# Gated cross-attention: the attended memory computed already turned, and softmax shares applied ahead of the turn

## The chip, the cores and the metric

The kernel runs on one core of a Trainium2 chip. The metric is the device time of one execution in microseconds (us). Three runs of the kernel before are shown by their median; a further, profiled execution has a time of its own.

## What is computed

For each of 32 batches there are 112 rows of `x` (512 numbers each) and 375 memory rows (256 numbers each).

```
memory_proj    = memory @ W_mem.T                          # 375 x 512
scores         = x @ memory_proj.T / sqrt(512)             # 112 x 375
attn           = softmax(scores)
memory_context = attn @ memory_proj                        # 112 x 512
gate           = sigmoid(concat(x, memory_context) @ W_gate.T + b_gate)
fused          = x + gate * memory_context
out            = fused * rsqrt(mean(fused**2) + 1e-6) * norm_w
```

The kernel never forms `memory_proj`. It computes q = x W_mem (112 x 256), scores = q memory.T, the attended memory am = attn memory (112 x 256), and from am both the context (am W_mem.T) and the gate's second half (am times a weight product made once).

## The kernel before, in words

Every operand of a product is split into two float32r parts, a rounded "high" and the remainder "low". A product is three kinds of matmul into one accumulator: high by high, high left by low right, and low left by high right. ScalarE (ACT) writes the high parts by a copy with rounding, VectorE (DVE) or GpSimd (POOL) writes the low ones by a subtraction. The left operand of `pe.matmul(out, left, right)` is the one that is loaded into TensorE (PE) and stays there; the right one streams through, one column after the other.

Work is done in 4 groups of 8 batches, the middle two in a hardware loop. The 896 rows of a group make 7 tiles of 128 rows for gate, context and output, and three column units (256, 320, 320) for q. There is no scheduler: each engine has its own written order of work, and semaphores join them. On PE, batch `b` of a group is

1. `score(b)`: 6 matmuls of 376 columns (done at the end of the group before for b = 0)
2. `after_scores`: fillers from `fillers(g, b, last)`, from b = 3 on `gate_x(b-1)`, 12 matmuls of 512 columns; 9 of them in the last batch of the last group
3. `probs_turn(b)`: 3 transposes of the exponentials (112 x 384) into the bank `pT_ps`
4. `after_probs`: fillers, from b = 2 on `gate_am(b-2)`, 6 matmuls of 512 columns
5. `attend(b)`: 9 matmuls. The left operand is a 128 x 112 block of the turned exponentials, the right one a 128 x 256 block of memory; the sum is am, 112 x 256, in `am_bank`
6. `after_am`: fillers, from b = 2 on `context(b-2)`, 6 matmuls of 512 columns
7. `am_turn(b)`: 2 transposes of am, which ACT has copied to SBUF and scaled by `share` (one over the row's sum), back into `am_bank`

On DVE the order of batch b is `gate_context(b-3)`, `amT_low(b-1)`, `maximum(b)` (row maximum and its scaling), `fuse(b-3)`, `shares(b)` (the reciprocal of the row sums), `pT_low(b)`, q remainders, `norm(b-3)`, `add_bias(b-2)`. Between groups it is ... `fuse(6)`, `maximum` of the next group's batch 0, a q remainder, `norm(6)`, and then the next group's `shares(0)`. ACT computes the exponential and its row sum, then a square, memory splits, `pT_hi`, `am`, a tanh and `amT_hi`. POOL computes the memory and x remainders and the inverse root for `norm`.

`probs_turn` waits for `probs_ready` (ACT's exponential) alone; `share` is needed only at the copy of am.

Of the kernel before, what the change touches and what calls it, by code (L numbers as in the profile page):

```python
# [24 lines left out]
F32R = mybir.dt.float32r  # L25
ACT = mybir.ActivationFunctionType
# [54 lines left out]
def build_gated_cross_attention(nc, x_d, xT_d, mems_d, first_d, wmT_d, wgT_d, b_d, nw_d, out_d):  # L81
    ctx = ExitStack()
    with ctx:
# [25 lines left out]
        memT_hi, memT_lo = (sb(f"memT_{s}", [P, 2, EC, KEVEN], F32R) for s in ("hi", "lo"))  # L109
        mem_hi, mem_lo = (sb(f"mem_{s}", [P, 2, KC, E], F32R) for s in ("hi", "lo"))  # L110
        probs = sb("probs", [ROWS, 2, KPAD])
        pT_hi, pT_lo = (sb(f"pT_{s}", [P, 2, KC, ROWS], F32R) for s in ("hi", "lo"))
        am = sb("am", [ROWS, E])
        x_rows = sb("x_rows", [P, X_SLOTS, D])
        work = sb("work", [P, 8, D])
        z, late_h, y = work[:, 0:2], work[:, 2:4], work[:, 4:6]
# [34 lines left out]
        late_ps = [ctx_ps, gate_ps[LAST_SLOT - 1]]  # L151
        scores = score_ps[0:ROWS, 0:KEVEN]
        probsT = pT_ps[:, 0:KC * ROWS].rearrange("p (c n) -> p c n", c=KC)
        am_ps = am_bank[0:ROWS, 0:E]
        amT_ps = am_bank[:, E:E + EC * ROWS].rearrange("p (c n) -> p c n", c=EC)


        wmT_loaded, vectors_loaded = sem("wmT_loaded"), sem("vectors_loaded")
# [19 lines left out]
        scores_done, top_ready, shift_ready = sem("scores_done"), sem("top_ready"), sem("shift_ready")  # L178
        probs_ready, share_ready = sem("probs_ready"), sem("share_ready")
        pT_done, pT_hi_ready, pT_lo_ready = sem("pT_done"), sem("pT_hi_ready"), sem("pT_lo_ready")  # L180
        am_done, am_ready = sem("am_done"), sem("am_ready")
        amT_done, amT_hi_ready, amT_lo_ready = sem("amT_done"), sem("amT_hi_ready"), sem("amT_lo_ready")
        gate_x_done, gate_done, ctx_done = sem("gate_x_done"), sem("gate_done"), sem("ctx_done")
        z_ready, tanh_ready, u_ready, h_ready = sem("z_ready"), sem("tanh_ready"), sem("u_ready"), sem("h_ready")
        meansq_ready, guarded_ready, rstd_ready = sem("meansq_ready"), sem("guarded_ready"), sem("rstd_ready")
# [89 lines left out]
        def _(pe):  # L275
# [50 lines left out]
                low_lefts(scores, q, memory).then_inc(scores_done, 1)  # L326

            def probs_turn(g, b):
                pe.wait_ge(probs_ready, GROUP * g + b + 1)
                for c in range(KC):  # L330
                    mm = pe.transpose(probsT[:, c], probs[:, b % 2, c * P:(c + 1) * P], ident[0:ROWS, 0:ROWS])  # L331
                mm.then_inc(pT_done, 1)

            def attend(g, b):
                turned = [(pT_hi[:, b % 2, c], pT_lo[:, b % 2, c]) for c in range(KC)]
                memory = [(mem_hi[:, b % 2, c], mem_lo[:, b % 2, c]) for c in range(KC)]
                pe.wait_ge(pT_hi_ready, GROUP * g + b + 1)
                pe.wait_ge(mem_hi_ready, GROUP * g + b + 1)
                pe.wait_ge(mem_lo_ready, GROUP * g + b + 1)
                if b > 0:  # L340

                    pe.wait_ge(amT_lo_ready, GROUP * g + b)
                high_lefts(am_ps, turned, memory)
                pe.wait_ge(pT_lo_ready, GROUP * g + b + 1)
                low_lefts(am_ps, turned, memory).then_inc(am_done, 1)

            def am_turn(g, b):
                pe.wait_ge(am_ready, GROUP * g + b + 1)
                for c in range(EC):
                    mm = pe.transpose(amT_ps[:, c], am[:, c * P:(c + 1) * P], ident[0:ROWS, 0:ROWS])  # L350
                mm.then_inc(amT_done, 1)

            def gate_x(g, t, part=WHOLE):
# [39 lines left out]
            def fillers(g, b, last):  # L393

                if b == 0:
                    return ([(q_piece, 1, 1)], [(gate_x, 0, OPEN)], [(q_piece, 2, 0, OPEN)])
                if b == 1:
                    return ([(q_piece, 2, 0, CLOSE), (gate_x, 0, CLOSE)], [(gate_x, 1, OPEN)], [(q_piece, 2, 1, OPEN)])
                if b == GROUP - 1 and last:
                    return ([(gate_x, b - 1, (0, 3))], [(gate_am, b - 2)], [(context, b - 2, OPEN)])  # L400
                gates = [(q_piece, 2, 1, CLOSE), (gate_x, 1, CLOSE)] if b == 2 else [(gate_x, b - 1)]
                return (gates, [(gate_am, b - 2)], [(context, b - 2)])

            def group(g, last, first=False):


                for b in range(GROUP):
                    after_scores, after_probs, after_am = fillers(g, b, last)
                    if first and b == 0:
                        after_scores = []  # L410
                    if b > 0:
                        score(g, b)
                    for what, *which in after_scores:
                        what(g, *which)
                    probs_turn(g, b)
                    for what, *which in after_probs:
                        what(g, *which)
                    attend(g, b)
                    for what, *which in after_am:
                        what(g, *which)  # L420
                    am_turn(g, b)
                if last:
                    context(g, TILES - 2, CLOSE)
                    gate_x(g, TILES - 1, (3, 4))
                    gate_am(g, TILES - 1)
                    for cols, bank in zip(HALVES, late_ps):
                        context(g, TILES - 1, cols=cols, bank=bank, late=True)
                else:
                    q_piece(g + 1, 0, 0)
                    q_piece(g + 1, 0, 1)  # L430
                    gate_am(g, TILES - 1)
                    context(g, TILES - 1)
                    score(g + 1, 0)
                    q_piece(g + 1, 1, 0)
# [72 lines left out]
        def _(act):  # L507
# [86 lines left out]
            def group(g, last, first=False):  # L594
                for b in range(GROUP):
                    ahead = not last or b + 1 < GROUP
                    after = (g, b + 1) if b + 1 < GROUP else (g + 1, 0)
                    if first and b == 1:
                        wga_high(0)
                    elif b > 0 and ahead:  # L600
                        split_memT(*after)
                    if b > 0:
                        exponentials(g, b)
                    if b >= 3:
                        square(g, b - 3)
                    if first and b == 1:
                        wga_high(1)
                    elif b > 0 and ahead:
                        split_mem(*after)
                    if b in (1, 2) and not (first and b == 1):  # L610
                        q_high(g, 2, b - 1)
                    act.wait_ge(pT_done, GROUP * g + b + 1)
                    high(pT_hi[:, b % 2], probsT).then_inc(pT_hi_ready, 1)
                    if first and b == 1:
                        split_memT(*after)
                        q_high(g, 2, 0)
                        wmT_high(0)
                    if b == 0:
                        if not first:
                            split_memT(*after)  # L620
                            q_high(g, 1, 1)
                        else:
                            wgx_high(2)
                            wgx_high(3)
                        split_mem(*after)
                    if not last and b in SPLIT_AT:

                        unit = SPLIT_AT.index(b)
                        act.wait_ge(gate_x_done, TILES * g + last_tile_of(unit) + 1)
                        split_xT(g + 1, unit)  # L630

                    act.wait_ge(share_ready, GROUP * g + b + 1)
                    act.wait_ge(am_done, GROUP * g + b + 1)
                    act.activation(am[:], am_ps, ACT.Copy,  # L634
                                   scale=share[:, b % 2:b % 2 + 1]).then_inc(am_ready, 1)
                    if b >= 2:
                        tanh(g, b - 2)
                    act.wait_ge(amT_done, GROUP * g + b + 1)
                    high(amT_hi[:, :, b * ROWS:(b + 1) * ROWS], amT_ps).then_inc(amT_hi_ready, 1)
                    if first and b == 1:  # L640
                        wmT_high(1)
                        split_mem(*after)
# [22 lines left out]
        def _(dve):  # L665
# [17 lines left out]
            def shares(g, b):  # L683
                s = slice(b % 2, b % 2 + 1)
                dve.wait_ge(probs_ready, GROUP * g + b + 1)
                dve.reciprocal(share[:, s], total[:, s]).then_inc(share_ready, 1)

            def pT_low(g, b):
                dve.wait_ge(pT_hi_ready, GROUP * g + b + 1)
# [2 lines left out]
            def amT_low(g, b):  # L692
                cols = slice(b * ROWS, (b + 1) * ROWS)
                dve.wait_ge(amT_hi_ready, GROUP * g + b + 1)
                low(amT_lo[:, :, cols], amT_ps, amT_hi[:, :, cols]).then_inc(amT_lo_ready, 1)

            def add_bias(g, t, cols=ALL):
                dve.wait_ge(vectors_loaded, 32)
# [85 lines left out]

            def group(g, last, first=False):
                for b in range(GROUP):
                    if b >= 3:
                        gate_context(g, b - 3)
                    if b >= 1:
                        amT_low(g, b - 1)  # L790
                    if b > 0:
                        maximum(g, b)
                    if first and b == 1:
# [23 lines left out]
                if last:  # L817
# [10 lines left out]
                    for cols in HALVES:  # L828
                        norm(g, TILES - 1, cols, late_h[:, LAST_SLOT])
                else:  # L830
                    gate_context(g, TILES - 2)
                    amT_low(g, GROUP - 1)
                    fuse(g, TILES - 2)
                    q_low(g + 1, 0, 0)
                    norm(g, TILES - 2)
# [123 lines left out]
```

## Time and profile before

| | |
|---|---|
| median of 3 runs | 299.44 us (297.44 to 299.56) |
| profiled execution, its own time | 297.53 us |
| its span, first to last instruction | 295.7 us |
| granted TensorE clock, mean over the span | 0.994 |
| PE matmuls | 287.5 us busy, 97% of the span, 1638 instructions |
| PE weight loads | 250.9 us, 85%, beside the matmuls |
| ACT / DVE / POOL busy | 59% / 53% / 53% |

Busy times are sums over the span. PE records overlap one another, since a matmul's record lasts until its results are out, so the spacing of their starts or of their ends is what they cost, not their duration. An engine that is half busy costs nothing unless PE waits for it.

### The profile page before, as it was taken

Reading aid. Unit: us, or ns where it says so; the run is one execution under the profiler, and the core shown is the slowest. Engines: PE = TensorE matmul, PEld = TensorE weight load, DVE = VectorE, ACT = ScalarE, POOL = GpSimd, SP = SyncE. Lnnn points to the kernel's source line nnn. Section 1 sums busy time; section 2 is a strip of 40 time slices with the busy share of each in tenths; the row PEclk is TensorE's granted clock in tenths of the full one; section 3 lists DMA queues with packets and bytes.
Section 4 is the critical chain, followed back from the end, with each engine's and each line's share of the span. In section 5 each row is a group of like instructions: output and inputs, shape, how many; then the busy total and the mean of one; then the engine's idle time right before and its main releaser. Section 6 shows DMA issues by size and latency. Waiting matters only on the chain.

```text
span 295.7 us, 4924 instructions
## 1 busy us (share of the span) xinstructions
PE 287.5 (97%) x1638; PEld 250.9 (85%) x1638; DVE 155.4 (53%) x327; ACT 173.1 (59%) x364; POOL 156.3 (53%) x132
## 2 busy tenths in 40 slices
PE   6999999999999999999999999999999999999991
PEld 3989888888989988888889988888889998888881
DVE  3897555455554255545464344555456334555555
ACT  4886657667537555657636555757744656555442
POOL 0002765858717545859824645775861954445302
PEclk9999999999999999999999999999999999999997
DMA  7997257576532734656561551757562333552101
GB/s 273 423 349 248 95 207 266 176 254 189 173 112 56 261 109 151 230 170 199 164 222 71 155 200 46 258 168 265 176 212 71 137 111 105 178 176 73 38 35 71
DMA packets 15426, 50.83 MB, mean 172 GB/s; under 512 B 1712, under 2 KB 1968, under 8 KB 15152
## 3 DMA queue, kind: packets, MB, share of 16 engines
q1 hardware_dynamic: 15408, 50.60, 50.7%
q8 instruction: 10, 0.16, 0.2%
q14 instruction: 8, 0.07, 0.1%
HBM read 43.25 MB, written 7.34 MB: 171 GB/s over the span
## 4 chain that ended last, share of the span: by engine, by line
PE 93%; DMA 3%; ACT 1%; DVE 1%; issue 0%; DVEq 0%; POOL 0%; POOLq 0%; SPq 0%
PE gate_ps L279 13%; PE gate_ps L281 13%; PE gate_ps L286 13%; PE ctx_ps L279 5%; PE ctx_ps L286 5%; PE ctx_ps L281 5%; PE am_bank L286 4%; PE am_bank L281 4%; PE am_bank L279 4%; PE q_ps L286 4%; PE q_ps L279 4%; PE q_ps L281 4%; PE score_ps L279 4%; PE score_ps L286 4%; PE score_ps L281 4%; PE pT_ps L331 3%
## 5 line engine op out<-in xcount | busy, mean ns | idle before, releaser
L853 POOL TENSOR_TENSOR memT_lo<-mems_raw,memT_hi 128x752 fp32r<-128x752 f32 x30 | 54.5, 1815 | 88.2 <-ACT memT_hi L509 88.2
L853 POOL TENSOR_TENSOR mem_lo<-mems_raw,mem_hi 128x768 fp32r<-128x768 f32 x30 | 56.4, 1881 | 3.5 <-ACT mem_hi L509 3.5
L634 ACT ACTIVATE am<-am_bank,share 112x256 f32<-112x256 f32 x32 | 15.2, 476 | 47.0 <-PE am_bank L286 47.0
L667 DVE TENSOR_TENSOR pT_lo<-pT_ps,pT_hi 128x336 fp32r<-128x336 f32 x32 | 16.2, 508 | 47.1 <-ACT pT_hi L509 47.0
L706 DVE SCALAR_TENSOR_TENSOR ctx_ps<-work,ctx_ps 128x512 f32<-128x512 f32 x26 | 18.1, 697 | 40.9 <-PE ctx_ps L286 40.9
L534 ACT ACTIVATE probs<-score_ps,shift 112x375 f32<-112x375 f32 x32 | 18.4, 575 | 27.5 <-DVE shift L681 27.5
L279 PE MATMUL gate_ps<-wgx_hi,xT_hi 128*128 128x512 f32 x112 | 32.4, 398 | 0.0
L281 PE MATMUL gate_ps<-wgx_lo,xT_hi 128*128 128x512 f32 x112 | 31.7, 392 | 0.0
L286 PE MATMUL gate_ps<-wgx_hi,xT_lo 128*128 128x512 f32 x112 | 31.6, 391 | 0.0
L509 ACT ACTIVATE memT_hi<-mems_raw 128x752 fp32r<-128x752 f32 x32 | 26.4, 826 | 0.9 <-DMA mems_raw<-in_mems 0.9
L509 ACT ACTIVATE mem_hi<-mems_raw 128x768 fp32r<-128x768 f32 x32 | 26.8, 837 | 0.0
L871 POOL TENSOR_TENSOR guarded<-meansq,eps 128x1 f32<-128x1 f32 x27 | 5.1, 191 | 39.9 <-ACT work L541 39.9
L853 POOL TENSOR_TENSOR xT_lo<-xT_raw,xT_hi 128x1280 fp32r<-128x1280 f32 (+1 forms) x9 | 25.0, 2776 | 0.0
L281 PEld LDWEIGHTS gate_ps<-wgx_lo,xT_hi 128*128 128x128 f32 x112 | 21.0, 188 | 4.6
L286 PEld LDWEIGHTS gate_ps<-wgx_hi,xT_lo 128*128 128x128 f32 x112 | 21.0, 188 | 4.6
L721 DVE SCALAR_TENSOR_TENSOR work<-ctx_ps,rstd,norm_w 128x512 f32<-128x512 f32 x26 | 19.4, 744 | 3.8 <-POOL rstd L873 3.7
L279 PEld LDWEIGHTS gate_ps<-wgx_hi,xT_hi 128*128 128x128 f32 x112 | 19.8, 188 | 1.8
L546 ACT ACTIVATE work<-work 128x512 f32<-128x512 f32 (+1 forms) x29 | 17.6, 610 | 5.9 <-DVE work L700 5.9
L509 ACT ACTIVATE amT_hi<-am_bank 128x224 fp32r<-128x224 f32 x32 | 11.5, 358 | 16.3 <-PE am_bank L350 16.3
L667 DVE TENSOR_TENSOR amT_lo<-am_bank,amT_hi 128x224 fp32r<-128x224 f32 x32 | 12.3, 386 | 15.9 <-ACT amT_hi L509 15.9
L679 DVE TENSOR_REDUCE top<-score_ps 112x1 f32<-112x375 f32 x32 | 17.5, 548 | 5.7 <-PE score_ps L286 5.7
L700 DVE TENSOR_TENSOR work<-gate_ps,b_gate 128x512 f32<-128x512 f32 (+1 forms) x29 | 19.2, 664 | 0.9 <-PE gate_ps L286 0.6
(128 smaller groups left out, 663.9 us busy)
## 6 DMA issues: line engine op xcount, KB each, us to landing
mems_raw<-in_mems SPq DMA_DIRECT2D x32, 760.0 KB, 4.5
x_rows<-in_x SPq DMA_DIRECT2D x28, 256.0 KB, 4.9
out<-work SPq DMA_DIRECT2D x27, 256.0 KB, 5.1
xT_raw<-in_xT SPq DMA_DIRECT2D x8, 640.0 KB, 5.7
xT_raw<-in_xT SPq DMA_DIRECT2D x3, 512.0 KB, 5.2
work<-in_wgT SPq DMA_DIRECT2D x1, 1024.0 KB, 7.7
x_rows<-in_wgT SPq DMA_DIRECT2D x1, 1024.0 KB, 10.8
first_raw<-in_first SPq DMA_DIRECT2D x1, 512.0 KB, 3.8
```

The lines of the kernel that those rows point to most:

```text
L279: pe.matmul(out, l_hi, r_hi, start=first and i == 0, stop=False)
L281: pe.matmul(out, l_hi, r_lo, start=False, stop=False)
L286: mm = pe.matmul(out, l_lo, r_hi, start=False, stop=last and i == len(lefts) - 1)
L509: return act.activation(out, in_, ACT.Copy)
L534: act.activation(probs[:, b % 2, 0:KEYS], scores[:, 0:KEYS], ACT.Exp, bias=shift[:, b % 2:b % 2 + 1], scale=D ** -0.5, accum_out=total[:, ...
L546: act.activation(z[:, t % 2, cols], z[:, t % 2, cols], ACT.Tanh, scale=0.5).then_inc(tanh_ready, 1)
L667: return dve.tensor_tensor(out, in_, high.bitcast(F32), ALU.subtract)
L679: dve.tensor_reduce(top[:, s], scores[:, 0:KEYS], AX.X, ALU.max).then_inc(top_ready, 1)
L700: dve.tensor_tensor(z[:, t % 2, cols], gate_ps[t % 2][:, cols], b_gate[:, cols], ALU.add).then_inc(z_ready, 1)
L706: dve.scalar_tensor_tensor(out=u[:, cols], in0=z[:, t % 2, cols], scalar=1.0, in1=bank[:, cols], op0=ALU.add, op1=ALU.mult).then_inc(u_rea ...
L721: dve.scalar_tensor_tensor(out=y[:, t % 2, cols], in0=h[:, cols], scalar=rstd[:, t % 2:t % 2 + 1], in1=norm_w[:, cols], op0=ALU.mult, op1= ...
L853: return pool.tensor_tensor(out, in_, high.bitcast(F32), ALU.subtract)
```

## The change

The attended memory is computed with memory as the left (loaded) operand, so it comes out as 256 x 112 already turned, in two blocks `e` of 128. The high and low turned exponentials stand side by side in one tile `pT`, so that one matmul by the high memory streams both, 224 columns; one by the low memory streams the high ones alone, 112 columns. Per batch these are 12 matmuls in place of 9, and `am_turn` with its copy on ACT is gone. The product by the low exponentials lies in a second part of the bank and is added by DVE: `amT_low` becomes two instructions. The division by the row sum moves ahead of the transposes: `shares` gets a DVE instruction that multiplies the 112 x 375 exponentials in place, and `probs_turn` waits for that. `attend` waits for the low parts of `pT` before its first matmul. Fillers of batches 1 and 2 are placed anew, and `amT_low` goes ahead of `gate_context` on DVE.

```
             def probs_turn(g, b):
-                pe.wait_ge(probs_ready, GROUP * g + b + 1)
+                pe.wait_ge(shared_ready, GROUP * g + b + 1)
...
             def attend(g, b):
-                pe.wait_ge(pT_hi_ready, GROUP * g + b + 1)
+                slot = b % 2
+                pe.wait_ge(pT_lo_ready, GROUP * g + b + 1)
...
-                high_lefts(am_ps, turned, memory)
-                pe.wait_ge(pT_lo_ready, GROUP * g + b + 1)
-                low_lefts(am_ps, turned, memory).then_inc(am_done, 1)
-
-            def am_turn(g, b):
-                pe.wait_ge(am_ready, GROUP * g + b + 1)
-                for c in range(EC):
-                    mm = pe.transpose(amT_ps[:, c], am[:, c * P:(c + 1) * P], ident[0:ROWS, 0:ROWS])
+                for e in range(EC):
+                    es = slice(e * P, (e + 1) * P)
+
+                    def by_high(c, first=False, last=False):
+                        return pe.matmul(amT_parts[:, e], mem_hi[:, slot, c, es], pT[:, slot, c], start=first, stop=last)
+
+                    def by_low(c):
+                        pe.matmul(amT_parts[:, e, 0], mem_lo[:, slot, c, es], pT[:, slot, c, 0], start=False, stop=False)
+
+                    by_high(0, first=True)
+                    for c in range(KC - 1):
+                        by_low(c)
+                        if c > 0:
+                            by_high(c)
+                    by_low(KC - 1)
+                    mm = by_high(KC - 1, last=True)
                 mm.then_inc(amT_done, 1)
...
                 if b == 1:
-                    return ([(q_piece, 2, 0, CLOSE), (gate_x, 0, CLOSE)], [(gate_x, 1, OPEN)], [(q_piece, 2, 1, OPEN)])
+                    return ([(q_piece, 2, 0, CLOSE), (gate_x, 0, CLOSE), (q_piece, 2, 1, OPEN)], [(gate_x, 1, OPEN)], [])
+                if b == 2:
+                    return ([(q_piece, 2, 1, CLOSE), (gate_x, 1, CLOSE), (gate_am, 0)], [(context, 0)], [])
...
-                gates = [(q_piece, 2, 1, CLOSE), (gate_x, 1, CLOSE)] if b == 2 else [(gate_x, b - 1)]
-                return (gates, [(gate_am, b - 2)], [(context, b - 2)])
+                return ([(gate_x, b - 1)], [(gate_am, b - 2)], [(context, b - 2)])
...
-                    act.wait_ge(share_ready, GROUP * g + b + 1)
-                    act.wait_ge(am_done, GROUP * g + b + 1)
-                    act.activation(am[:], am_ps, ACT.Copy,
-                                   scale=share[:, b % 2:b % 2 + 1]).then_inc(am_ready, 1)
...
                 dve.reciprocal(share[:, s], total[:, s]).then_inc(share_ready, 1)
+                dve.wait_ge(share_ready, GROUP * g + b + 1)
+                dve.tensor_scalar(probs[:, b % 2, 0:KEYS], probs[:, b % 2, 0:KEYS], share[:, s], None,
+                                  ALU.mult).then_inc(shared_ready, 1)
...
-                low(amT_lo[:, :, cols], amT_ps, amT_hi[:, :, cols]).then_inc(amT_lo_ready, 1)
+                low(amT_rest[:], amT_ps, amT_hi[:, :, cols]).then_inc(amT_rest_ready, 1)
+                dve.wait_ge(amT_rest_ready, GROUP * g + b + 1)
+                dve.tensor_tensor(amT_lo[:, :, cols], amT_rest[:], amT_parts[:, :, 1], ALU.add).then_inc(amT_lo_ready, 1)
...
                 for b in range(GROUP):
+                    if b >= 1:
+                        amT_low(g, b - 1)
                     if b >= 3:
                         gate_context(g, b - 3)
-                    if b >= 1:
-                        amT_low(g, b - 1)
```

## Rows read from the trace of the kernel before

**Rows 1.** The page, chain that ended last: shares of the span by engine.

```profile
PE 93%; DMA 3%; ACT 1%; DVE 1%; issue 0%; DVEq 0%; POOL 0%; POOLq 0%; SPq 0%
```

**Rows 2.** The chain in order of time, 158 to 163 us: start, us, what.

```profile
158.32 0.29 PE pT_ps L331 x3
...
160.01 0.35 PE am_bank L279 x3
...
161.94 0.20 PE am_bank L350 x2
```

**Rows 3.** Weight loads in time, 158.0 to 162.3 us: start, us of the run, count.

```profile
157.87 0.19 PEld L286 LDWEIGHTS q_ps<-xT_hi,wm_lo 128*128 128x128 f32 x1
...
158.36 0.30 PEld L279 LDWEIGHTS gate_ps<-wgx_hi,xT_hi 128*128 128x128 f32 x2
```

**Rows 4.** The chain in order of time, 146 to 149 us.

```profile
147.83 0.49 PE q_ps L279 x4
```

**Rows 5.** All engines in time, a steady batch (b = 4), 185.7 to 190.4 us.

```profile
185.99 0.55 DVE L679 TENSOR_REDUCE top<-score_ps 112x1 f32<-112x375 f32 x1 [0.16 <-PE score_ps L286]
186.13 1.81 POOL L853 TENSOR_TENSOR memT_lo<-mems_raw,memT_hi 128x752 fp32r<-128x752 f32 x1 [3.32 <-ACT memT_hi L509]
186.57 0.15 DVE L681 TENSOR_SCALAR shift<-top 112x1 f32<-112x1 f32 x1
...
187.46 0.16 DVE L686 RECIPROCAL share<-total 112x1 f32<-112x1 f32 x1
...
188.56 0.45 PE L331 MATMUL pT_ps<-ident,probs 112*128 112x112 f32 x3
...
189.53 0.51 DVE L667 TENSOR_TENSOR pT_lo<-pT_ps,pT_hi 128x336 fp32r<-128x336 f32 x1 [1.91 <-ACT pT_hi L509]
...
190.25 0.40 PE L279 MATMUL am_bank<-mem_hi,pT_hi 128*112 128x256 f32 x2
```

**Rows 6.** All engines in time, start of a group, 158.0 to 159.4 us.

```profile
158.16 0.45 PE L331 MATMUL pT_ps<-ident,probs 112*128 112x112 f32 x3
158.32 0.75 DVE L721 SCALAR_TENSOR_TENSOR work<-ctx_ps,rstd,norm_w 128x512 f32<-128x512 f32 x1 [0.18 <-POOL rstd L873]
...
158.99 0.15 DVE L686 RECIPROCAL share<-total 112x1 f32<-112x1 f32 x1
```

**Rows 7.** All engines in time, batches 2 and 3, 174 to 181 us.

```profile
174.75 0.52 PE L286 MATMUL am_bank<-mem_hi,pT_lo 128*112 128x256 f32 x3
...
176.74 0.69 DVE L706 SCALAR_TENSOR_TENSOR ctx_ps<-work,ctx_ps 128x512 f32<-128x512 f32 x1 [1.80 <-PE ctx_ps L286]
...
177.34 0.38 DVE L667 TENSOR_TENSOR amT_lo<-am_bank,amT_hi 128x224 fp32r<-128x224 f32 x1
...
180.45 0.45 PE L331 MATMUL pT_ps<-ident,probs 112*128 112x112 f32 x3
```

**Rows 8.** All engines in time, first group, 18 to 34.5 us.

```profile
18.81 0.45 PE L331 MATMUL pT_ps<-ident,probs 112*128 112x112 f32 x3
...
19.53 0.15 DVE L686 RECIPROCAL share<-total 112x1 f32<-112x1 f32 x1
...
25.92 0.45 PE L331 MATMUL pT_ps<-ident,probs 112*128 112x112 f32 x3
...
26.57 0.15 DVE L686 RECIPROCAL share<-total 112x1 f32<-112x1 f32 x1
...
27.75 1.81 POOL L853 TENSOR_TENSOR memT_lo<-mems_raw,memT_hi 128x752 fp32r<-128x752 f32 x1 [26.27 <-ACT memT_hi L509]
...
28.46 1.66 DVE L667 TENSOR_TENSOR wmT_lo<-first_raw,wmT_hi 128x512 fp32r<-128x512 f32 x1
...
31.67 0.68 DVE L667 TENSOR_TENSOR wmT_lo<-first_raw,wmT_hi 128x512 fp32r<-128x512 f32 x1
...
33.32 0.51 PE L331 MATMUL pT_ps<-ident,probs 112*128 112x112 f32 x3
```

**Rows 9.** All engines in time, last batch, 281.0 to 282.5 us.

```profile
281.26 0.16 DVE L686 RECIPROCAL share<-total 112x1 f32<-112x1 f32 x1
...
281.68 0.45 PE L331 MATMUL pT_ps<-ident,probs 112*128 112x112 f32 x3
```

More of the change, by code:

```diff
@@ L111, in build_gated_cross_attention @@
         probs = sb("probs", [ROWS, 2, KPAD])
-        pT_hi, pT_lo = (sb(f"pT_{s}", [P, 2, KC, ROWS], F32R) for s in ("hi", "lo"))
-        am = sb("am", [ROWS, E])
+        pT = sb("pT", [P, 2, KC, 2, ROWS], F32R)
+        pT_hi, pT_lo = pT[:, :, :, 0], pT[:, :, :, 1]
+        amT_rest = sb("amT_rest", [P, EC, ROWS])
         x_rows = sb("x_rows", [P, X_SLOTS, D])
@@ L153, in build_gated_cross_attention @@
         probsT = pT_ps[:, 0:KC * ROWS].rearrange("p (c n) -> p c n", c=KC)
-        am_ps = am_bank[0:ROWS, 0:E]
-        amT_ps = am_bank[:, E:E + EC * ROWS].rearrange("p (c n) -> p c n", c=EC)
+        amT_parts = am_bank[:, 0:EC * 2 * ROWS].rearrange("p (c s n) -> p c s n", c=EC, s=2)
+        amT_ps = amT_parts[:, :, 0]
         wmT_loaded, vectors_loaded = sem("wmT_loaded"), sem("vectors_loaded")
@@ L180, in build_gated_cross_attention @@
         pT_done, pT_hi_ready, pT_lo_ready = sem("pT_done"), sem("pT_hi_ready"), sem("pT_lo_ready")
-        am_done, am_ready = sem("am_done"), sem("am_ready")
-        amT_done, amT_hi_ready, amT_lo_ready = sem("amT_done"), sem("amT_hi_ready"), sem("amT_lo_ready")
+        shared_ready, amT_done, amT_rest_ready = sem("shared_ready"), sem("amT_done"), sem("amT_rest_ready")
+        amT_hi_ready, amT_lo_ready = sem("amT_hi_ready"), sem("amT_lo_ready")
         gate_x_done, gate_done, ctx_done = sem("gate_x_done"), sem("gate_done"), sem("ctx_done")
@@ L334, in attend @@
             def attend(g, b):
-                turned = [(pT_hi[:, b % 2, c], pT_lo[:, b % 2, c]) for c in range(KC)]
-                memory = [(mem_hi[:, b % 2, c], mem_lo[:, b % 2, c]) for c in range(KC)]
-                pe.wait_ge(pT_hi_ready, GROUP * g + b + 1)
+                slot = b % 2
+                pe.wait_ge(pT_lo_ready, GROUP * g + b + 1)
                 pe.wait_ge(mem_hi_ready, GROUP * g + b + 1)
@@ L420, in group @@
                         what(g, *which)
-                    am_turn(g, b)
                 if last:
@@ L830, in group @@
                 else:
+                    amT_low(g, GROUP - 1)
                     gate_context(g, TILES - 2)
-                    amT_low(g, GROUP - 1)
                     fuse(g, TILES - 2)
```

## The prediction, as it went on record

> **What bounds the kernel now.** The first view to read is the chain that ended last: 93% of the span is PE [rows 1]. The second is that chain in order of time, which shows PE's groups of work back to back: three transposes in 0.29 us, three attending matmuls in 0.35 us, two transposes of am in 0.20 us [rows 2]. So a PE matmul costs its spacing (0.117 us for an attending one, 0.10 for a transpose), and whatever lengthens PE's stream or makes PE wait lengthens the kernel. The third view is the timeline of all engines at the places where the change adds a wait: there the question is how long before PE's transposes the reciprocal of the row sums is done [rows 5, 6, 8, 9].
>
> **PE's own stream.** Removed per batch: 9 attending matmuls, 3 x 0.35 = 1.05 us, and 2 transposes, 0.20 us [rows 2], together 1.25 us. Added: 12 matmuls, 6 of 224 and 6 of 112 columns. In columns this is a gain: 2016 in place of 2304 plus 224. But all twelve need a new load of 128 columns. The loads are the limit: two loads that stand directly behind one another take 0.30 us where one takes 0.19 [rows 3], so a load starts no sooner than 0.11 us after the one before it, whatever streams beside it. The matmuls of the q product that stream 256 columns past a 128-column load come every 0.49 / 4 = 0.12 us [rows 4]. A 224-column matmul lies near that row, a 112-column one near the bare load; I take the middle, 0.115, so 12 x 0.115 = 1.38 us, or +0.13 per batch and +4.2 us for 32. The bounds are 12 x 0.11 = 1.32 (+2.2 us in all) and 12 x 0.12 = 1.44 (+6.1 us).
>
> The spacing in rows 3 speaks against what a page would let one hope. The Trainium skill, "TensorE: Matmul & The Clock Gate", section "Back-to-back issue gap", gives about 81 ns per matmul for a sustained stream of load and matmul pairs at 128 columns. With that for the six narrow ones and 0.11 for the others the attending would take 1.15 us, a gain of 3.3 us in all; the two loads of this trace stand at 0.11 us, and I go by them.
>
> **The multiply ahead of the transposes.** The trace has no such instruction (112 x 375, SBUF to SBUF, a scalar per row). From below its cost is that of a one-column one, 0.15 us; from above that of the reduction over the same 375 columns, 0.55 us [rows 5]. I take the upper one, since its size is the same. Add 0.03 between two dependent DVE instructions (186.54 to 186.57 [rows 5]) and 0.11 from a release to the first transpose: I estimate that as 0.05 for the semaphore and 0.06 for a load that can't be hidden, since the run of three at 33.32, which came straight out of a wait, has 0.51 us and not 0.45 [rows 8, 5]. So the first transpose can come no sooner than 0.69 us after the end of the reciprocal.
>
> The Trainium skill, "VectorE: DVE Perf Modes", section "Mode 2x_2P", says that a float32 tensor_scalar from SBUF takes two elements per cycle. As an estimate from that page's 0.96 GHz this makes 0.15 + 0.20 = 0.35 us, and the whole sum 2.0 us less; no row here shows it.
>
> - Steady batches (4 to 7 of a group, and batch 7 in all but the last): the reciprocal ends at 187.62, so the transposes may start at 188.31; they start at 188.56 [rows 5]. Cost 0, with 0.25 to spare. The cover is the 2.8 us of `gate_x`; without it every batch would wait. If DVE and POOL exclude each other while this multiply runs, it starts at POOL's end, 187.94, and the transposes at 188.60, 0.04 late. That such a hold exists is in the first group: one DVE subtraction of two SBUF tensors took 1.66 us and its twin 0.68, the long one while POOL was in an instruction until 29.56 [rows 8].
> - Start of groups 1 to 3: the transposes now run at 158.16, before `share` exists. DVE is in `norm(6)` from 158.32 to 159.07, which waited for POOL, and the reciprocal ends at 159.14 [rows 6]. New start 159.83, so PE waits 1.67 us, three times: 5.0 us. Queued behind PE's wait are the gate's first half and `attend`, nothing that could run instead.
> - Batch 0 of the first group: reciprocal done at 19.68 (DVE is in x's remainder before it), transposes at 18.81 [rows 8]; new 20.37, 1.6 us.
> - Batch 1 of the first group: reciprocal done 26.72, transposes 25.92 [rows 8]; the moved q filler (6 matmuls of 320 columns, 6 x 0.12 x 320 / 256 = 0.90 us by rows 4) puts PE's arrival at 26.82, and the new start is 27.41: 0.6 us. Batches 1 and 2 of later groups get 0.9 and 1.39 us more cover than they had and don't wait.
> - Batch 3, all groups: `context(0)` no longer stands between `attend(2)` and `score(3)`, and `amT_low(2)`, now twice 0.38, with `gate_context(0)`, 0.69 [rows 7], stands before `maximum(3)` on DVE. With `attend(2)` ending 0.33 later, at 175.60, PE reaches the transposes at 175.60 + 1.03 (score) + 2.77 (gate) - 0.16 (overlap of records) = 179.24. DVE: 0.05 and 0.36 for ACT's `amT_hi`, then 0.04 + 0.38 + 0.03 + 0.38 - 0.08 + 0.69 - 0.06, maximum 0.55, 0.03 and 0.15, exponential with its sum 0.81, reciprocal 0.03 + 0.16 ends at 179.13. Transposes at 179.82: 0.6 us, four times 2.3 us.
> - Last batch, with 9 gate matmuls as cover: reciprocal done 281.42, transposes 281.68 [rows 9]; new 282.11, 0.4 us.
> - The third batch of the first group now waits some 0.3 us for its exponential; its longer cover gives that back: -0.3.
>
> Waits together: 5.0 + 1.6 + 0.6 + 2.3 + 0.4 - 0.3 = 9.6 us.
>
> **Other parts.** `attend` waits for `pT_lo` at its head: it is done at 190.04 and the first matmul comes at 190.25 [rows 5]. Its load must start some 0.11 before that, so 0.1 is left; cost 0, and at most 0.05 x 32 = 1.6 us if a release takes longer. ACT's copy of am (0.48 us) was hidden behind context, and its going gives nothing; `amT_hi` comes earlier. DVE's second `amT_low` instruction falls, outside batch 3, into the time in which DVE waited for PE (1.67 to 1.9 us idle ahead of `gate_context` and `pT_lo`) [rows 5, 7]: 0. ACT's memory split at the start of a group stands behind `pT_hi` and so comes 1.67 us later, but so does everything of PE behind it: 0. No DMA is added or removed.
>
> **The sum.** 297.5 (the profiled execution's own time, 1.8 above its span) + 4.2 + 9.6 = 311.3 us. That execution lies 1.9 us under the median and at the low end of the three runs, so a median may come out up to 2 us higher.
>
> **Rivals.**
> - Columns decide, not loads. If the 0.11 us in rows 3 is a start-up effect and a stream of loads hides behind narrow matmuls, each costs its columns: 2016 x 0.455 ns (0.35 us for 3 x 256 columns in rows 2) = 0.92 us per batch in place of 1.25, -10.6 us. With the waits: 297.5 - 10.6 + 9.6 = 296.5, not slower. It decides from the point where a 112-column matmul follows another in clearly less than 0.11 us. Against it: every load in rows 3 starts only when the matmul before its own has started, and the two of the pair are 0.11 apart. Chance 0.10.
> - Narrow float32r matmuls stream slower. Every one of the kernel before has 256 columns or more; the only 112-column stream, the transposes, takes 0.097 us, 0.86 ns per column against 0.455 [rows 2]. At that rate 224 columns take 0.19, 112 stay at the load's 0.11: 1.83 us per batch, +18.6, or 325.7 us. A page has a harsher case: the Trainium skill, "FP8 and Floating Point Precision", section "TensorE Precision Notes", gives true float32 four passes; by four passes at 0.455 ns a batch would take 3.7 us and the kernel some 385. For it stands only that row; against it, that a transpose is another kind of work and that the wide matmuls show one rate from 256 to 512 columns. Chance 0.12.
> - The waits are smaller: the multiply costs near 0.15 us, at ten places 0.4 less each, and loads go at 0.11. 297.5 + 2.2 + 5.6 = 305.3. Chance 0.2, on the same side as the forecast.
> - The forecast itself, 307 to 318: 0.55. Its upper end holds 0.12 us for each matmul (+1.9), POOL's hold in the steady batches and the later `pT_lo` (+2), and the higher median (+2). Something else: 0.03.
>
> **How the numbers follow.** Predicted 311.3. The range 304 to 318 takes in the forecast and the small waits (0.75), and leaves out the two others. What a measurement of this kernel can tell from no change is about 1%. Faster by over 1% needs the column rival and a cheap multiply: 0.06. Within 1%: the rest of that rival: 0.07. Slower: 0.87.
>
> **What the changed profile would show.** The attending matmuls' ends 0.11 to 0.12 us apart, alike for 224 and 112 columns (right), or 0.05 and 0.10 in turn (columns), or 0.19 and more (slow narrow streams). A wait of PE at the transposes released by DVE's multiply: about 1.7 us at three group starts, 1.6 and 0.6 in the first group, 0.6 in each batch 3, none in batches 4 to 6. The multiply's own duration, 0.15 to 0.55. The prediction is wrong above all if the multiply is not behind `norm(6)` in time, or if the spacing of narrow matmuls is not the load's.

## The result, and the profile after

The kernel after takes 311.48 us (median of 4 runs, 310.81 to 312.57) against 298.76 us (4 runs) for the one before: 1.043 times the time [1.038, 1.049]. The prediction was 311.3. Its profiled execution took 310.81 us with a span of 308.9, so that the difference between the two profiled executions is 13.3 us, where the prediction had 13.8 (4.2 in PE's stream, 9.6 in waits). Some 0.5 us of the 13.3 lies ahead of everything that was changed: PE reaches its first transposes at 19.45 us, in the profiled execution of the kernel before at 18.97.

The page of the kernel after, busy time and share of the span of each engine, then the shares of the chain that ended last:

```profile
PE 292.9 (95%) x1670; PEld 253.7 (82%) x1670; DVE 184.8 (60%) x391; ACT 157.8 (51%) x332; POOL 155.7 (50%) x132
...
PE 80%; DVE 10%; issue 3%; ACT 2%; POOL 2%; DMA 1%; DVEq 0%; POOLq 0%; ACTq 0%
```

PE's busy time grew by 5.4 us, but its share of the chain fell from 93% [rows 1] to 80%, and DVE's rose from 1% to 10%. The chain now runs through DVE wherever PE waits for a multiply; DVE's busy share over the whole span (60%) would never have told that.

**The attending.** The chain in order of time, a steady batch of the kernel after (start, us, what):

```profile
206.96 0.29 PE pT_ps L332 x3
...
208.65 0.10 PE am_bank L347
208.75 0.17 PE am_bank L350 x2
208.92 0.17 PE am_bank L347
209.09 0.06 PE am_bank L350
...
209.82 0.16 PE am_bank L347
209.98 0.47 PE ctx_ps L280 x2
```

L347 streams 224 columns, L350 streams 112. The ends look as if the wide ones took 0.16 us and the narrow ones 0.06. That is the records' ends alone: all twelve fill 208.65 to 209.98, 1.33 us, or 0.111 each, which is the spacing of two loads in rows 3. Before, the attending and the transposes of am took 1.25 us [rows 2]. The whole steady batch grew from 8.09 us (three transposes at 188.72 and again at 196.81) to 8.18 (198.78 to 206.96): 0.09 in each of 32, some 2.8 us.

**The start of a group.** All engines in time (start, us, engine, line, and in brackets the idle time of the engine before it and what ended it):

```profile
166.04 0.75 DVE L730 SCALAR_TENSOR_TENSOR work<-ctx_ps,rstd,norm_w 128x512 f32<-128x512 f32 x1 [0.18 <-POOL rstd L882]
166.71 0.15 DVE L690 RECIPROCAL share<-total 112x1 f32<-112x1 f32 x1
...
166.90 0.41 DVE L692 TENSOR_SCALAR probs<-probs,share 112x375 f32<-112x375 f32 x1
...
167.37 0.51 PE L332 MATMUL pT_ps<-ident,probs 112*128 112x112 f32 x3 [1.33 <-DVE probs L692]
```

`norm(6)` stands first on DVE, the reciprocal and the multiply right behind it, and PE has nothing to do meanwhile. By the spacing of the matmuls (a record outlasts it, so the bracket says a little less) PE lost 1.55 us here, 1.43 and 1.55 in the two other groups, and 1.51 in batch 0 of the first.

**Batch 3.** The same view, where PE is released last by the end of DVE's whole list:

```profile
187.54 0.69 DVE L715 SCALAR_TENSOR_TENSOR ctx_ps<-work,ctx_ps 128x512 f32<-128x512 f32 x1
...
188.90 0.57 ACT L542 ACTIVATE probs<-score_ps,shift 112x375 f32<-112x375 f32 x1 [1.40 <-DVE shift L685]
188.90 0.70 DVE L722 SCALAR_TENSOR_TENSOR ctx_ps<-ctx_ps,x_rows 128x512 f32<-128x512 f32 x1
...
189.59 0.17 DVE L690 RECIPROCAL share<-total 112x1 f32<-112x1 f32 x1
...
189.79 0.42 DVE L692 TENSOR_SCALAR probs<-probs,share 112x375 f32<-112x375 f32 x1
...
190.26 0.51 PE L332 MATMUL pT_ps<-ident,probs 112*128 112x112 f32 x3
```

From 187.54 DVE has no gap. PE loses 0.34 us at the transposes here and in the groups before and behind this one, 0.57 in the first.

**A wait that the prediction did not have** is in the first group. All engines in time:

```profile
31.18 1.80 POOL L862 TENSOR_TENSOR memT_lo<-mems_raw,memT_hi 128x752 fp32r<-128x752 f32 x1 [29.70 <-ACT memT_hi L517]
...
33.12 0.57 PE L280 MATMUL score_ps<-memT_hi,qT_hi 128*112 128x376 f32 x2 [0.59 <-POOL memT_lo L862]
...
35.07 1.60 DVE L671 TENSOR_TENSOR wmT_lo<-first_raw,wmT_hi 128x512 fp32r<-128x512 f32 x1
...
36.08 2.25 POOL L862 TENSOR_TENSOR memT_lo<-mems_raw,memT_hi 128x752 fp32r<-128x752 f32 x1
...
36.78 1.76 DVE L692 TENSOR_SCALAR probs<-probs,share 112x375 f32<-112x375 f32 x1
...
38.60 0.51 PE L332 MATMUL pT_ps<-ident,probs 112*128 112x112 f32 x3 [0.60 <-DVE probs L692]
```

`score(2)` waits for POOL's low part of its memory, 0.82 us of spacing. Before, `am_turn(1)` and a q filler of 0.90 us stood ahead of it; the filler now runs ahead of the transposes of batch 1. The second loss, 0.82 us again, is the multiply of batch 2: it took 1.76 us and ended at 38.54, 0.21 after POOL's instruction beside it. That instruction was itself late: DVE's subtraction `wmT_lo` was running when it started, and it took 2.25 us where it usually takes 1.8. The subtraction in turn took 1.60 us where its twin took 0.68 [rows 8], since it started beside an earlier instruction of POOL that ended at 36.13. So a chain of such holds between DVE and POOL stands behind this wait. The view of the tile `probs` on DVE (duration of one in ns: least, median, greatest) has this as the greatest of the 32:

```profile
L692 DVE TENSOR_SCALAR probs<-probs,share x32: 414/416/1762, 20.2 to 294.4; 112x375 f32<-112x375 f32 x32
```

### The profile page after: what moved, and what is told of

It is laid out like the page before. It is cut to its first block, busy times and chain, and to the rows that moved or that the text cites. A ratio compares the mean times of both kernels' runs of the same rounds, so it can differ in the third digit from the quotient of the medians.

```text
span 308.9 us, 4988 instructions
## 1 busy us (share of the span) xinstructions
PE 292.9 (95%) x1670; PEld 253.7 (82%) x1670; DVE 184.8 (60%) x391; ACT 157.8 (51%) x332; POOL 155.7 (50%) x132
## 4 chain that ended last, share of the span: by engine, by line
PE 80%; DVE 10%; issue 3%; ACT 2%; POOL 2%; DMA 1%; DVEq 0%; POOLq 0%; ACTq 0%
PE gate_ps L280 11%; PE gate_ps L282 11%; PE gate_ps L287 11%; PE am_bank L347 9%; PE am_bank L350 5%; PE ctx_ps L280 5%; PE ctx_ps L282 4%; PE ctx_ps L287 4%; PE pT_ps L332 4%; PE score_ps L280 3%; PE score_ps L287 3%; PE score_ps L282 3%; PE q_ps L280 2%; PE q_ps L287 2%; PE q_ps L282 2%
## 5 line engine op out<-in xcount | busy, mean ns | idle before, releaser
L347 PE MATMUL am_bank<-pT,mem_hi 128*128 128x224 f32 x192 | 47.5, 309 | 0.0
L671 DVE TENSOR_TENSOR pT<-pT_ps,pT 128x336 fp32r<-128x336 f32 x32 | 16.2, 508 | 46.0 <-ACT pT L517 46.0
L347 PEld LDWEIGHTS am_bank<-pT,mem_hi 128*128 128x128 f32 x192 | 34.1, 191 | 4.3 <-DVE pT L671 0.9
L350 PE MATMUL am_bank<-pT,mem_lo 128*128 128x112 f32 x192 | 35.7, 240 | 0.0
L671 DVE TENSOR_TENSOR amT_rest<-am_bank,amT_hi 128x224 f32<-128x224 f32 x32 | 12.5, 391 | 31.9 <-ACT amT_hi L517 31.8
L350 PEld LDWEIGHTS am_bank<-pT,mem_lo 128*128 128x128 f32 x192 | 31.6, 191 | 0.0
L517 ACT ACTIVATE pT<-pT_ps 128x336 fp32r<-128x336 f32 x32 | 14.4, 450 | 24.6 <-PE pT_ps L332 24.0
L332 PEld LDWEIGHTS pT_ps<-ident,probs 112*128 112x128 f32 x96 | 11.2, 140 | 13.2 <-DVE probs L692 9.1
```

Of the source, the lines that this page charges most:

```text
L347: return pe.matmul(amT_parts[:, e], mem_hi[:, slot, c, es], pT[:, slot, c], start=first, stop=last)
L350: pe.matmul(amT_parts[:, e, 0], mem_lo[:, slot, c, es], pT[:, slot, c, 0], start=False, stop=False)
L517: return act.activation(out, in_, ACT.Copy)
L671: return dve.tensor_tensor(out, in_, high.bitcast(F32), ALU.subtract)
```

## The experiments

All are edits of the kernel after unless said otherwise. The kernel before, measured beside them in three series, had medians of 298.81, 298.03 and 299.2 us; the ratios are to these. A "wait" below is what the spacing of PE's matmuls exceeds their usual one.

**A start of two lengths.** Profiled times must be compared with care, since the first 10 us can differ. Matmuls of 256 columns in the kernel after, then in the kernel below that has its shares first (start, us of two, count):

```profile
8.38 0.40 PE L452 MATMUL pT_ps<-xT_lo,wm_hi 128*128 128x256 f32 x2
8.62 0.40 PE L452 MATMUL am_bank<-xT_lo,wm_hi 128*128 128x256 f32 x2
```

```profile
8.50 0.63 PE L452 MATMUL pT_ps<-xT_hi,wm_hi 128*128 128x256 f32 x2
8.93 0.63 PE L452 MATMUL am_bank<-xT_hi,wm_hi 128*128 128x256 f32 x2
```

They come 0.12 us apart in the first and 0.21 in the second. PE then reaches its first transposes at 20.5 to 20.9 us (multiply alone, wide low matmuls, shares first, no low memory), in all the others at 19.0 to 19.7. These edits touch nothing of PE's work there; what causes it is not shown.

**One half alone: the attending.** The multiply is left out, so the output is not divided by the row sums.

```
-                pe.wait_ge(shared_ready, GROUP * g + b + 1)
+                pe.wait_ge(probs_ready, GROUP * g + b + 1)
...
-                dve.wait_ge(share_ready, GROUP * g + b + 1)
-                dve.tensor_scalar(probs[:, b % 2, 0:KEYS], probs[:, b % 2, 0:KEYS], share[:, s], None,
-                                  ALU.mult).then_inc(shared_ready, 1)
```

> The changed kernel without the multiply by the row share (the exponentials go into the transposes undivided, so the output is not normalised); PE's transposes wait for the exponential again. Theory of weight loads and waits: the attending matmuls keep 0.111 us spacing, PE's stream is 0.08 us per batch longer than in the kernel before (+2.4 us in all), the head of attend waits for the low turned exponentials a little (+0.4), all waits at the transposes go except in batch 3; about 301 us in a profile against 297.5. Rival, the waits come from the new attend and the refilled order and not from the multiply: 308 us or more.

Measured: 302.79 us, 1.014 [1.009, 1.019]. No wait at any transposes is left. `score(2)` of the first group still waits 0.81, and at the head of `attend(3)` PE now waits 0.28 to 0.42 us for `pT_lo`, since it gets there earlier. So its 4.0 us are some 2.8 of PE's stream and, for the rest, these waits.

**One half alone: the multiply,** put into the kernel before, with its old attending, its old copy of am (now without the scale) and its old fillers.

```
-                pe.wait_ge(probs_ready, GROUP * g + b + 1)
+                pe.wait_ge(shared_ready, GROUP * g + b + 1)
...
-                    act.wait_ge(share_ready, GROUP * g + b + 1)
...
-                    act.activation(am[:], am_ps, ACT.Copy,
-                                   scale=share[:, b % 2:b % 2 + 1]).then_inc(am_ready, 1)
+                    act.activation(am[:], am_ps, ACT.Copy).then_inc(am_ready, 1)
...
+                dve.wait_ge(share_ready, GROUP * g + b + 1)
+                dve.tensor_scalar(probs[:, b % 2, 0:KEYS], probs[:, b % 2, 0:KEYS], share[:, s], None,
+                                  ALU.mult).then_inc(shared_ready, 1)
```

> The kernel before with the multiply ahead of the transposes as the only change (the copy of am no longer scales). Theory of waits: 1.4 us at each of four group starts, 1.4 us in batch 1 of the first group, some 0.4 us in batches 1 and 2 of the later groups where POOL is in a memory split when the multiply would start, 0.3 us in the last batch, together some 10 us: about 308 us. Rival, PE's stream absorbs the waits because work behind it was ready anyway: under 302 us.

Measured: 309.31 us, 1.034 [1.029, 1.039]. All engines in time in batch 1 of a later group:

```profile
172.27 1.82 POOL L855 TENSOR_TENSOR memT_lo<-mems_raw,memT_hi 128x752 fp32r<-128x752 f32 x1
...
173.67 0.63 DVE L687 TENSOR_SCALAR probs<-probs,share 112x375 f32<-112x375 f32 x1
```

The same wait at the group starts (1.44, 1.55, 1.55, and 1.50 in batch 0 of the first), and in place of the kernel after's small ones 1.37 and 1.28 us in batches 1 and 2 of the first group, 0.34 to 0.38 and 0.18 in those of the others. The multiply alone thus costs 10.5 us by the medians and the attending alone 4.0; together they cost 12.7, since the moved fillers cover batches 1 and 2. In the steady batches too this kernel's multiply starts beside POOL: it takes 0.47 to 0.50 us and PE does not wait for it.

**Columns or loads.** The matmuls by the low memory stream the low exponentials too, 224 columns in place of 112, so the second part of the sum also holds low by low.

```
-                        pe.matmul(amT_parts[:, e, 0], mem_lo[:, slot, c, es], pT[:, slot, c, 0], start=False, stop=False)
+                        pe.matmul(amT_parts[:, e], mem_lo[:, slot, c, es], pT[:, slot, c], start=False, stop=False)
```

> The changed kernel with the six matmuls by the low memory streaming all 224 columns instead of 112 (they add the low by low product too). If weight loads set the spacing, the twelve still come 0.111 us apart and the time stays within 0.5 us of the changed kernel. If columns set it, 6 x 112 x 0.455 ns = 0.31 us per batch, +9.8 us.

Measured: 311.65 us, 1.042 [1.037, 1.047], within 0.2 us of the kernel after with 21,504 columns more. The chain in order of time:

```profile
209.88 0.11 PE am_bank L347
209.98 0.22 PE am_bank L350 x2
```

With equal columns the alternating ends are gone, and the spacing is 0.11 as in the kernel after. From PE's arrival at its first transposes to the end both kernels take 289.5 us. The columns cost nothing.

**Twice the loads for the same columns.** Each matmul of 224 columns by the high memory is cut into two of 112, with the same left operand.

```
-                        return pe.matmul(amT_parts[:, e], mem_hi[:, slot, c, es], pT[:, slot, c], start=first, stop=last)
+                        pe.matmul(amT_parts[:, e, 0], mem_hi[:, slot, c, es], pT[:, slot, c, 0], start=first, stop=False)
+                        return pe.matmul(amT_parts[:, e, 1], mem_hi[:, slot, c, es], pT[:, slot, c, 1], start=False, stop=last)
```

> The changed kernel with each 224-column matmul cut into two of 112 columns by the same left operand: 18 loads per batch for the same columns. If loads set the spacing, 6 x 0.111 = 0.67 us more per batch, 21 us in all: 332 us. If columns or a fixed rate per matmul column set it, no change: 311 us. If a repeated left operand is not loaded again, the matmul count rises but not the loads, and the time stays near 311 as well; the load count in the trace tells these two apart.

Measured: 332.21 us, 1.117 [1.112, 1.121]. Groups of weight loads by line (busy us, mean ns), then the chain in time:

```profile
L348 PEld LDWEIGHTS am_bank<-pT,mem_hi 128*128 128x128 f32 x192 | 36.7, 191 | 0.0
L347 PEld LDWEIGHTS am_bank<-pT,mem_hi 128*128 128x128 f32 x192 | 36.7, 191 | 4.4 <-DVE pT L672 1.0
```

```profile
222.33 0.11 PE am_bank L347
222.44 0.11 PE am_bank L348
```

L347 and L348 have the same left operand and a load each: it is loaded again (18 loads a batch), and 192 more matmuls cost 20.7 us: 0.108 each with not one column more. Matmuls and loads were added together, so this does not tell a load's price from a matmul's.

**Half the loads gone.** The six matmuls by the low memory are left out, and with them that part of the product.

```
                     by_high(0, first=True)
-                    for c in range(KC - 1):
-                        by_low(c)
-                        if c > 0:
-                            by_high(c)
-                    by_low(KC - 1)
+                    by_high(1)
                     mm = by_high(KC - 1, last=True)
```

> The changed kernel without the six matmuls by the low memory (that part of the product is left out). If each load costs 0.111 us, attending falls from 1.33 to 0.67 us per batch, 21 us less: 290 us, unless the shorter attending uncovers a wait. If columns set the price, 6 x 112 x 0.455 ns = 0.31 us per batch, 10 us less: 301 us.

Measured: 295.46 us, 0.987 [0.982, 0.991], 15.3 us under the kernel after by profiled times. The chain in order of time:

```profile
199.40 0.66 PE am_bank L347 x6
```

Six matmuls of 224 columns take 0.66 us, 0.11 each, so the stream did lose 192 x 0.111 = 21.3 us. The size of the whole was missed: the start took 1.5 us longer in this profiled execution, and 4.7 us came back as waits, since the same chains of ACT, DVE and POOL now had less of PE's work as cover. PE's waits add up to 16.0 us against 11.3 (0.81 at each batch 3, 1.05 in the first group, 1.50 at its `score(2)`, 0.55 at each `score(1)` of the others).

**The order on DVE at the group start.** Reciprocal and multiply of the next batch 0 go right behind its `maximum`, ahead of the q remainder and of `norm(6)`; in the first group they go ahead of the x remainder.

```
+            shares(0, 0)
...
-                    shares(g, b)
+                    if b > 0:
+                        shares(g, b)
...
+                    shares(g + 1, 0)
```

> The changed kernel with the reciprocal and the multiply of a group's first batch placed right behind its row maximum on DVE, ahead of a q remainder and the norm of the last tile (in the first group: ahead of the x remainder). Theory of waits: PE's waits at the first transposes of the four groups, 1.4 to 1.5 us each, go: 310.8 - 5.9 = about 305 us. Rival, what is pushed back by the multiply (norm, q remainder) becomes the next wait: 308 us or more.

Measured: 306.14 us, 1.024 [1.019, 1.029]. All engines in time at a group start:

```profile
163.02 0.16 DVE L690 RECIPROCAL share<-total 112x1 f32<-112x1 f32 x1 [0.73 <-ACT probs L542]
163.22 0.42 DVE L692 TENSOR_SCALAR probs<-probs,share 112x375 f32<-112x375 f32 x1
...
164.29 0.38 PEld L332 LDWEIGHTS pT_ps<-ident,probs 112*128 112x128 f32 x3
...
164.60 0.75 DVE L730 SCALAR_TENSOR_TENSOR work<-ctx_ps,rstd,norm_w 128x512 f32<-128x512 f32 x1 [0.18 <-POOL rstd L885]
```

The multiply is done at 163.64, 0.65 us before PE's first load, and `norm(6)` waits for POOL as it did. Waits of 6.0 us shrank to 0.11; the profiled time fell by 4.6 only, since its start took 1.3 us longer. So most of the wait half of the loss is one place in DVE's written order.

**The order on DVE in batch 3.** On top of that, `maximum(3)` ahead of `gate_context(0)`.

```
+                    if b == 3:
+                        maximum(g, b)
...
-                    if b > 0:
+                    if b > 0 and b != 3:
```

> The kernel with shares first at the group starts, and in batch 3 the row maximum ahead of gate_context on DVE. Theory of waits: PE's waits at the transposes of batch 3 (0.54 us in the first group, 0.33 in the three others) go, -1.5 us: 304.7 us in a profile. What stays above the kernel before is PE's longer attending, the waits of the first group's batches 1 and 2 and the waits at the head of attend; so it doesn't reach 300. Rival, PE's spacing was never the matter and it falls to that of the kernel before: under 300.

Measured: 305.58 us, 1.027 [1.022, 1.031], not to be told from the one before it. The expectation failed: the wait stayed at 0.32 us in three groups and grew from 0.54 to 0.78 in the first. All engines in time:

```profile
183.87 0.70 DVE L715 SCALAR_TENSOR_TENSOR ctx_ps<-work,ctx_ps 128x512 f32<-128x512 f32 x1
183.98 0.57 ACT L542 ACTIVATE probs<-score_ps,shift 112x375 f32<-112x375 f32 x1 [0.81 <-DVE shift L685]
...
184.67 0.70 DVE L722 SCALAR_TENSOR_TENSOR ctx_ps<-ctx_ps,x_rows 128x512 f32<-128x512 f32 x1
...
185.28 0.15 DVE L690 RECIPROCAL share<-total 112x1 f32<-112x1 f32 x1
```

The exponential's sum is there at 184.64 and the reciprocal begins at 185.28: the same two 0.7 us instructions still stand ahead of it. The work ahead of it had only been put in another order.

**So the fuse goes behind the shares** in batch 3, on top of that again.

```
-                    if b >= 3:
+                    if b > 3:
                         fuse(g, b - 3)
                     if b > 0:
                         shares(g, b)
+                    if b == 3:
+                        fuse(g, b - 3)
```

> The kernel with shares and maximum first, and in batch 3 also the reciprocal and the multiply ahead of fuse on DVE. If what PE waits for in batch 3 is the sum of DVE's work ahead of the multiply, taking fuse (0.7 us) from in front of it ends the wait of 0.32 us in three groups and most of 0.78 in the first: 305.2 - 1.7 = 303.5 us in a profile. Rival, the wait is for the exponential's row sum, which no order on DVE brings forward: no change, 305 us.

Measured: 308.15 us, 1.030 [1.026, 1.035], a miss in sign too. All engines in time:

```profile
186.65 0.69 DVE L722 SCALAR_TENSOR_TENSOR ctx_ps<-ctx_ps,x_rows 128x512 f32<-128x512 f32 x1
...
187.13 0.45 PE L332 MATMUL pT_ps<-ident,probs 112*128 112x112 f32 x3
...
187.37 0.60 ACT L549 ACTIVATE work<-ctx_ps 128x512 f32<-128x512 f32 x1 [1.29 <-DVE ctx_ps L722]
...
187.96 0.84 ACT L517 ACTIVATE mem_hi<-mems_raw 128x768 fp32r<-128x768 f32 x1
...
188.69 0.44 ACT L517 ACTIVATE pT<-pT_ps 128x336 fp32r<-128x336 f32 x1
...
189.72 0.19 PEld L347 LDWEIGHTS am_bank<-pT,mem_hi 128*128 128x128 f32 x1 [1.18 <-DVE pT L671]
```

The transposes of batch 3 wait no longer, but `attend(3)` does, 1.0 to 1.27 us. ACT's square waits for the fuse, and it stands on ACT ahead of a memory split and of `pT_hi`; the transposes were done 1.1 us before `pT_hi` began at 188.69. The wait moved over ACT's order and grew.

**The old orders with the new attending.** Fillers of batches 1 and 2 and `amT_low` on DVE as before the change.

```
-                    return ([(q_piece, 2, 0, CLOSE), (gate_x, 0, CLOSE), (q_piece, 2, 1, OPEN)], [(gate_x, 1, OPEN)], [])
...
+                    return ([(q_piece, 2, 0, CLOSE), (gate_x, 0, CLOSE)], [(gate_x, 1, OPEN)], [(q_piece, 2, 1, OPEN)])
...
-                    if b >= 1:
-                        amT_low(g, b - 1)
...
+                    if b >= 1:
+                        amT_low(g, b - 1)
```

> The changed kernel with the fillers of PE and the order of amT_low and gate_context of the kernel before. Theory of waits: batch 3 waits no more for its reduced cover (-1.6 us), but batches 1 and 2 wait as in the kernel with the multiply alone (+0.35 and +0.2 us in three groups, more in the first), and in batches 3 to 7 the longer amT_low now stands between gate_context and the row maximum, worth up to 0.15 us each: 311 to 314 us, so the new order gains little or nothing by itself and costs nothing. Rival, the new order is what made the change slow: under 306.

Measured: 315.5 us, 1.059 [1.054, 1.064]. The new orders are worth 4 us; they are no part of the loss. Without them `context(6)` waits 0.67 to 0.71 us in three groups where it waited 0.23 to 0.29, and the last transposes 0.67 where it was 0.31. In the first group, all engines in time; then the view of stretches (length, PE busy, granted clock, DMA share, GB/s) and the chain:

```profile
36.22 2.23 POOL L861 TENSOR_TENSOR memT_lo<-mems_raw,memT_hi 128x752 fp32r<-128x752 f32 x1
...
36.93 1.73 DVE L691 TENSOR_SCALAR probs<-probs,share 112x375 f32<-112x375 f32 x1
...
38.72 0.51 PE L332 MATMUL pT_ps<-ident,probs 112*128 112x112 f32 x3 [1.84 <-DVE probs L691]
```

```profile
36.00:38.70 2.70, 0.88 (x4) 1.00 0.51 138
38.70:41.70 3.00, 2.98 (x10) 0.57 1.00 339
```

```profile
39.23 0.87 PE gate_ps L280 x2
```

The multiply ended 0.21 us after POOL's instruction, PE waited 2.06 us, and then ran six 512-column matmuls 0.43 us apart where 0.23 is usual: the granted clock fell from 1.00 to 0.57 (the 1.2 GHz level for most of the stretch), 1.2 us more.

**A wait that both kernels have.** `context(6)` waits 0.23 to 0.29 us three times in both. In the kernel before, ACT's square goes ahead of the q copy that stood before it.

```
-                    q_high(g + 1, 0, 0)
                     square(g, TILES - 2)
+                    q_high(g + 1, 0, 0)
```

> The kernel before with one ACT step moved: at the end of a group the square of tile 5 ahead of the copy of q's first piece, so that norm(5) and with it context(6) come earlier. PE waits 0.24 to 0.28 us there in three groups; if these go it is 0.7 us faster, a quarter of a per cent, at the edge of what can be told. Rival, the copy of q that is pushed back makes its own wait: no gain.

Measured: 297.93 us against 298.03, 0.999 [0.996, 1.002]. In the trace these waits fell to 0.07 us at most, but 0.7 us of 298 is not shown by the times. No version here that computes the whole product beats the kernel before by an amount that can be told.

## Why the prediction was right

The time was 311.48 where 311.3 was said, and by its steps:

- **PE's stream**, said to cost 4.2 us (bounds 2.2 and 6.1). It cost 2.8: twelve matmuls at 0.111 us, near the lower bound, and not at 0.115. That their number sets the time and not their columns is shown three ways, with columns doubled at no cost, matmuls added at 0.108 each and matmuls removed at 0.111. The rival by columns (296.5 us) and the one by a slow narrow stream (325.7) both fall. That it is the load of each matmul, as the prediction has it, and not another fixed price of it, is not shown: in all these kernels every matmul has a load of its own. And "whatever streams beside it" was too wide, since the transposes load 128 columns too and come every 0.097 us [rows 2]. The Trainium skill, "TensorE: Matmul & The Clock Gate", section "Back-to-back issue gap", would have about 81 ns for such a matmul; this case's 112-column ones come every 111 ns, and the measurement decides.
- **The multiply** was taken at 0.55 us from the reduction over the same columns, between 0.15 and 0.55. It took 0.416 at the median. The estimate from the Trainium skill, "VectorE: DVE Perf Modes", section "Mode 2x_2P", was 0.35: nearer than my row, and still 0.07 low. Each wait that hangs on the multiply alone is some 0.13 us smaller.
- **Group starts**: said 3 x 1.67, measured 1.43, 1.55, 1.55. Batch 0 of the first group: 1.6 and 1.51. Batch 1: 0.6 and 0.49. Last batch: 0.4 and 0.31. The mechanism, `norm(6)` ahead of the reciprocal, is shown by the kernel that changes only that order.
- **Batch 3**: said 4 x 0.6 = 2.3 us, measured 0.57 and 3 x 0.34 = 1.6, at the place and through the chain foretold. What the sum did not see is that `fuse(0)` ends at the same moment as the exponential (189.59), so that either alone keeps the wait; and the multiply is 0.13 cheaper.
- **Batch 2 of the first group**: said -0.3, measured +0.5 (a wait of 0.82 where the kernel before has 0.30). That POOL can hold a DVE instruction was in the prediction, from rows 8, but only for the steady batches, and there the multiply of the kernel after never runs beside POOL's splits.
- **`score(2)` of the first group**, 0.82 us, was missed. The filler moved out from before it was counted where it went, not where it had been.
- **The head of `attend(3)`**, said 0 to 0.05, waits 0.20 once and 0.10 twice.
- **Steady batches**: no wait, as said. At 205.92 the multiply starts and at 206.80 the transposes, by the profile, with 0.35 us to spare.

PE's waits add up to 11.3 us against 1.3 before: 10.0, where 9.6 was said. Upward go two misses of 0.8 us in the first group and 0.4 at `attend(3)`; the cheaper multiply and batch 3 go downward. With 2.8 for the stream and 0.5 for the longer start, which is no part of the change, that is the 13.3 us. So the mechanism and its places were right, but that the forecast came within 0.2 us is luck: its errors, up to 1.4 us each, offset one another.

One slip stands in the chances: "the rest of that rival" is given 0.07, but 0.10 less 0.06 leaves 0.04; the other 0.03 can only be that of "something else".

## What to carry to other kernels

Count matmuls, each with its left operand, as well as columns: at 112 and 224 columns their number set the time here, and the swap of operands, which took away columns, made 12 of what had been 11 with the transposes. A step put between two engines was free in the steady batches; it must be priced at group starts, first and last batches, by the written order of its engine. When fillers move, look at both ends of the move; and before an instruction is put behind another, follow who waits for it on the next engine.

## What the runs showed of the hardware

- A DVE instruction whose operands lie in SBUF can be held until POOL's running one ends: the multiply of 0.42 us took 1.76, 1.73 and 0.63 us beside POOL's subtraction and ended 0.21 us after it each time. It goes the other way too: POOL's subtraction took 2.25 and 2.23 us in place of 1.8 where it started beside DVE's `wmT_lo`. A DVE subtraction that reads PSUM, and the one-column reciprocal, took their usual 0.49 (at 31.36) and 0.15 us (at 36.60) beside POOL's. More than these rows was not tried.
- A matmul with the left operand of the one before it has it loaded again (192 more loads in the profile).
- Behind a wait of 2.06 us on PE the granted clock was 0.57 over the next 3 us; waits of 1.4 to 1.55 us in the other kernels left it at full. One case, not repeated.
- The first 256-column matmuls of an execution came 0.12 us apart in some profiled executions and 0.21 in others, up to some 10 us.
- The ends of matmul records can alternate, 0.16 and 0.06, while the stream goes at an even 0.111.
